# Fourteen instead of twelve of 125 edge tiles take their source columns by copies

## The reference, cut to what matters

```
h_nodes = silu(x @ Wn1 + bn1) @ Wn2 + bn2
h_edges = silu(edge_attr @ We1 + be1) @ We2 + be2
msgs = silu(concat[h_nodes[dst], h_nodes[src], h_edges] @ Wm1 + bm1) @ Wm2 + bm2
agg = segment_sum(msgs, dst) / max(counts, 1)
out = layernorm(x + upd) * g + b,   upd = silu(concat[x, agg] @ Wu1 + bu1) @ Wu2 + bu2
result = layernorm(x + out)
```

## Time and profile before

| | |
|---|---|
| median of the runs | 3641.66 us |
| profiled execution | 3643.69 us, span 3641.8 |
| GpSimd busy | 2698.5 us (74%) |
| VectorE busy | 2735.3 us (75%) |
| ScalarE busy | 2995.1 us (82%) |
| TensorE busy | 2794.5 us (77%), granted clock 0.76 on average |
| chain that ended last | GpSimd 64%, issue 21% |

### The profile page before, as it was taken

How to read it: one execution, slowest core, us unless ns; L and a number is a source line. 1 busy time by engine, 2 the same in 40 slices (tenths; PEclk the granted TensorE clock), 3 DMA queues, 4 the chain that set the end, 5 groups by cost and what they waited for, 6 DMA issues and landing times.

```text
span 3641.8 us, 93892 instructions
## 1 busy us (share of the span) xinstructions
PE 2794.5 (77%) x16224; PEld 2174.9 (60%) x16224; DVE 2735.3 (75%) x20847; ACT 2995.1 (82%) x23073; POOL 2698.5 (74%) x2848
## 2 busy tenths in 40 slices
PE   4878778777877788787777778777777787887785
PEld 2666556555666566666655556565655565665564
DVE  4778778778678677777687787786787877777876
ACT  3998888888888888888888888888888888888885
POOL 4777777777777777777777777777777777777774
PEclk7777777778777777777687787777777777677776
DMA  7444444444444444444454444444444444444442
GB/s 218 95 100 98 86 91 95 94 101 95 92 98 87 92 100 91 98 101 87 88 103 86 100 95 94 97 89 89 101 91 98 101 88 93 88 94 100 95 94 44
DMA packets 257330, 350.11 MB, mean 96 GB/s; under 512 B 105688, under 2 KB 193069, under 8 KB 246862
## 3 DMA queue, kind: packets, MB, share of 16 engines
q1 hardware_dynamic: 163340, 245.92, 31.8%
q0 software_dynamic: 91424, 95.97, 14.3%
q10 hardware_dynamic: 1954, 2.14, 0.2%
HBM read 330.76 MB, written 13.01 MB: 94 GB/s over the span
## 4 chain that ended last, share of the span: by engine, by line
POOL 64%; issue 21%; PE 8%; DMA 4%; DVE 2%; ACT 0%; DVEq 0%; SPq 0%; POOLq 0%; ACTq 0%
POOL b_ring L800 64%; DMA b_ring<-b_table,src 4%; PE p_pre L686 2%; PE p_pre L692 2%; PE p_sum L706 1%; PE p_hid L815 1%; DVE colbuf L632 1%; DMA work<-in_xT 1%; PE p_pre L695 0%; DVE comb L902 0%; PE p_last L958 0%; PE p_hid L378 0%; PE p_last L959 0%; DMA b_table<-to_ab 0%; DVE stats L995 0%
## 5 line engine op out<-in xcount | busy, mean ns | idle before, releaser
L800 POOL DMA_INDIRECT b_ring<-b_table,src x2825 | 2676.1, 947 | 865.8 <-issue 850.2
L632 ACT COPY colbuf<-shared 64x4 uint8 x21134 | 2128.0, 190 | 152.1 <-issue 140.7
L632 DVE COPY colbuf<-shared 64x4 uint8 x17511 | 1375.4, 194 | 282.2 <-issue 275.6
L686 PE MATMUL p_pre<-wa_ring,comb 128*128 128x64 f32 x6250 | 1027.7, 325 | 0.0
L686 PEld LDWEIGHTS p_pre<-wa_ring,comb 128*128 128x128 f32 x6250 | 979.2, 241 | 1.0 <-issue 1.0
L692 PE MATMUL p_pre<-b_ring,ident 128*128 128x320 f32 (+1 forms) x1250 | 575.3, 552 | 490.8 <-DMA b_ring<-b_table,src 488.3
L717 ACT ACTIVATE comb<-p_hid,b_e 64x320 f32<-64x320 f32 x1250 | 652.8, 522 | 359.8 <-PE p_hid L815 346.4
L902 DVE SCALAR_TENSOR_TENSOR comb<-shared,p_const 64x640 f32<-64x640 int32 x625 | 554.1, 887 | 506.2 <-PE p_pre L686 420.8
L706 PEld LDWEIGHTS p_sum<-hot_ring,msg 128*65 128x65 f32 x6250 | 579.8, 178 | 476.5 <-DVE agg L912 280.7
L706 PE MATMUL p_sum<-hot_ring,msg 128*65 128x64 f32 x6250 | 641.3, 267 | 278.4 <-DVE agg L912 171.6
L692 PEld LDWEIGHTS p_pre<-b_ring,ident 128*128 128x128 f32 x1250 | 295.5, 250 | 691.1 <-DMA b_ring<-b_table,src 577.2
(11 more groups left out here) (106 smaller groups left out, 592.4 us busy)
## 6 DMA issues: line engine op xcount, KB each, us to landing
e_ring<-in_edgeT SPq DMA_DIRECT2D x250, 320.0 KB
shared<-in_dst_row SPq DMA_DIRECT2D x125, 640.0 KB
b_ring<-b_table,src POOLq DMA_INDIRECT x2825
e_ring<-in_edgeT SPq DMA_DIRECT2D x50, 400.0 KB
shared<-in_dst_row SPq DMA_DIRECT2D x25, 800.0 KB
wa_ring<-a_table SPq DMA_DIRECT2D x625, 16.0 KB
work<-in_xT SPq DMA_DIRECT2D x25, 250.0 KB
work<-in_x SPq DMA_DIRECT2D x25, 250.0 KB
```

Of the source, the lines that this page charges most:

```text
L632: end = copy(colbuf[:, special % COLBUF, at:at + 1].bitcast(U8), of[j])
L686: return eng.matmul(p_pre[:, i % 2, k * H:(k + 1) * H], comb[:, i % COMBS, k * P:(k + 1) * P], wa_ring[:, i % RING, :], start=k == 0, stop ...
L800: eng.indirect_dma_start(b_ring[:, b_slot(i), k, :], None, b_table, bass.IndirectOffsetOnAxis(ap=src[:, u * TILES + k:u * TILES + k + 1], ...
```

## The change

SPECIAL has 14 units of a round instead of 12; of a special tile's 128 columns VectorE copies 61 instead of 58 and ScalarE 67 instead of 70. colbuf has 7 slots instead of 4, and VectorE's list has room for 40 words a unit instead of 32. In VectorE's loop the load of the list and the copies are done in two parts, the one-hot (hot) and the addition standing between them; before, both one-hots stood first, then one load and all copies, then the addition.

```diff
-SPECIAL = [1, 3, 5, 7, 9, 11, 13, 15, 17, 19, 21, 23]
-COLS = dict(vector=58, scalar=70)
-COLBUF = 4
+SPECIAL = [1, 2, 4, 6, 8, 9, 11, 13, 15, 17, 18, 20, 22, 24]
+COLS = dict(vector=61, scalar=67)
+COLBUF = 7
 LEADIN = 4
 HALF_AT = 13
 LIST_AT = (21, 8)
-LOAD = dict(vector=32, scalar=40)
+LOAD = dict(vector=40, scalar=40)
...
                 comb_of(i + AHEAD)
-            hot_of(i)
             if j in (0, HALF_AT):
                 wait_alone(eng, list_in[j // HALF_AT], 32 * rr + 32)
-            starts_v = loaded_columns(eng, "vector", j + LEADIN)
-            copied_columns(eng, "vector", eng.tensor_copy, j + LEADIN, starts_v).then_inc(col_ok["vector"], 1)
+            starts_v = loaded_columns(eng, "vector", j + LEADIN, 0, 2)
+            copied_columns(eng, "vector", eng.tensor_copy, j + LEADIN, starts_v, 0, 2)
+            hot_of(i)
             if i >= ADD_LAG:
                 add_sums(i - ADD_LAG)
+            starts_v = loaded_columns(eng, "vector", j + LEADIN, 1, 2)
+            copied_columns(eng, "vector", eng.tensor_copy, j + LEADIN, starts_v, 1, 2).then_inc(col_ok["vector"], 1)
             step(i)
```

## The result

The changed kernel takes 3695.51 us (median of four runs, 3693.84 to 3696.32), the kernel before beside it 3641.15. The ratio is 1.0148, with an interval from 1.0131 to 1.0166: slower by 54 us. I had forecast 3583, faster by 59 us, and a range up to 3622. Both the sign and the range were wrong.

What follows compares the result with a forecast made beforehand. GpSimd's row of 2825 gathers at 1.251 us was taken as the bound. From the profiled 3643.7 us, -62.5 for 50 gathers and +3 at the end gave 3584.2, stated as 3583 against the median; range 3577 to 3622.

Steps and rivals of the forecast that it cites:

- gaps 0.4: 4.67 us: VectorE's unit: comb 0.89, hot 0.49, addition 0.22, copies 2.68 and 0.4 us of load gaps make 4.67 us.
- 4.27 to 5.47: Bounds on VectorE's time a unit in us, with load gaps from 0 to 1.2 us; a round of 123.8 to 153.8.
- break-even: Round time of the other engines, 137.8 us, above which they pass GpSimd's span of 3579 and each us costs 25.
- 0.88 for "faster": Chance that the whole kernel gets faster: 0.70 forecast, 0.16 rival 1 or part of rival 2, 0.02 rival 3.
- -62.5 us: On GpSimd, 50 gathers fewer at 1.251 us each, all on the path while GpSimd waits for nobody.
- 134 + 25 r: Kernel time if the other engines need r us a round: start at about 102 us, 25 rounds, 38 at the end.
- Rival 1: VectorE's two list loads show, 0.63 us of gap a unit, r = 139.5: 3622 us; chance 0.16 with part of rival 2.
- Rival 2: ScalarE and VectorE take turns setting the pace, neither working ahead: 141.9 us a round, 3682 us; in full or with rival 1, 0.07 slower, 0.05 same.
- TensorE's slow units: TensorE's units of 6.1 us at a granted clock of 0.50, over GpSimd's 5.56; expected to be made good.
- The leads: 25 and 16 more copies ahead of the loop delay TensorE's first unit 2 to 3 us, hidden from GpSimd.
- The end's +3: At the last unit ScalarE and VectorE may be 0 to 10 us behind; 3 us added.
- Rival 3: GpSimd's gathers get dearer beside more VectorE copies; 1% growth gives back 35 us, 3618 us; chance 0.02.

Runs made afterwards that it cites:

- two experiments: The changed kernel with six copies a unit fewer on VectorE, 3605.48 us; and with VectorE's second load cut to four words, all copies kept, 3603.39 us.
- 57 and 71: The changed kernel with 57 of 128 columns on VectorE and 71 on ScalarE instead of 61 and 67: 3640.20 us; with the update also spread, 3616.77 us.

## Why the prediction was wrong, step by step

**The step that failed** is "gaps 0.4: 4.67 us" for VectorE's unit. Measured is (142.95 - 17)/25 = 5.04 us: inside the 4.27 to 5.47 that I had bounded, and above the break-even, 137.8 less 17 over 25, 4.83. The mechanism was in the sum, and the term is mis-sized in two parts. The gap was 431.6/625 = 0.69 us, not 0.4. A copy took 1743.9/21486 = 81.2 ns, not 78.5: 34.16 x 2.7 ns = 0.09. Together 0.38, which is the difference of 0.37 but for rounding. I had taken 0.44 from the earlier trace rows as the nearest row, but that is the average for one load of 28 words, and of an engine that waited 420.8 us for TensorE and so didn't set the pace. What tells of one that does is its gap behind comb and the price of a load by its words: two loads of 1.35 + 1.10 us, address arithmetic seven times 0.09 (the records of VectorE's queue), and 37 instructions to push at some 0.04 us (an estimate from the spaces between those records) come to about 4.6 us a unit in the sequencer. The engine's own work is 4.4 (0.89, 0.49, 0.21 and 34.16 x 0.0812). Neither hides the other in full: in the two places counted, the sequencer was six and eight instructions ahead when a load started. Together they make 5.04.

The chances failed with it. With half of the bounds (4.83 to 5.47) beyond the break-even, 0.88 for "faster" was not what my own bounds said. Their upper end, 153.8 us a round, gives 134 + 3845 = 3979, and my range stopped at 3622.

**Sum, term by term.** The gathers' -62.5 us was right in mechanism and size, and shows wherever VectorE gets out of the way (139.8 a round in two experiments, 27 of 31 us for thirteen tiles). Then the time comes back. The first of ScalarE's update activations moved from 281.3 to 288.6 us, the last from 3618.9 to 3670.6: 7 us in the first round and 44 in the other 24, 52 in all, which is the difference of the spans. With r = 142.95 my 134 + 25 r gives 3708, 14 above the span. It counts the update once too often: no update falls into the first round, and the last one runs alone in the 38 us at the end. With 17 us less it gives 3691, against 3693.4. So the break-even is r = 138.5 and not 137.8 (4.86 us a unit), and rivals 1 and 2 should have read 3605 and 3665.

**ScalarE** was right: busy 3251 us (3240 forecast), a unit 5.1 us between its activations (2007.46 to 2012.55), its longer load hidden. The Trainium skill's figure of 8 queued instructions (Advanced Engine Details and Errata, section Engine Queue Depths) I had weighed on ScalarE, where it changed little. The traces bear it out where it counts: VectorE's load at 2007.2 starts with seven unfinished copies and comb ahead of its first user, and in the run with the load ahead of comb six unfinished copies covered it. Weighed on VectorE it would have spoken against this change.

**TensorE, the leads, the end.** TensorE's slow units did not set the pace: with VectorE out of the way the rounds went at GpSimd's. The leads cost nothing: TensorE's first identity product runs at 99.34 us, 99.30 before. The end's +3 has no meaning with another bound.

**Rival 1** (VectorE's two loads show) is what happened, at a higher price: 0.69 of gap, not 0.63, and dearer copies; 3622 was forecast for it and 3695 measured. I had given it and a part of rival 2 a chance of 0.16, and only up to 3634. **Rival 2** had a number close by (3682), for a reason that the changed kernel doesn't have: with 8 copies a unit fewer on ScalarE the round stays at 142.9. Its mechanism exists at 57 and 71. **Rival 3** fell: 947 ns a gather, with 23% more copies on VectorE going on beside them. The Trainium skill (GPSIMD Engine Reference, section Specifications) speaks of contention between the two where VectorE's instruction is in a 2-port mode or has two inputs in SBUF. More copies beside the gathers brought none; whether a copy is of that kind no run here shows.

**What was to show it.** x2775 gathers at 1.25 us: yes. GpSimd's waits under 10 us: no, 103. TensorE's waits for gathers: none left. VectorE's issue before copies: 431.6 us, over the 0 to 400 that I gave, and its busy time 3123.7, not 3045. "Wrong if GpSimd waits for p_pre by tens of us; then r is over 138, and the engine without idle time names the rival": that is how it came, but for one word. VectorE has idle time in the page's sense, 20 us of the round; it has none that it waits for another.

**What stays open.** How much of the changed kernel's loss is the new order's (one load and one block of copies were not tried with 14 tiles at 61 and 67), how much the update's lumps add at that share, and what made six runs 29% slower.

## What to carry to other kernels

Give an engine's sequencer a row of its own in the sum: loads into registers, address arithmetic and the pushing of many tiny instructions. An engine that is 85% busy and waits for no one can be at its limit, as VectorE was here, and a gap that you read while it still had slack can grow when the slack is gone: 0.44 us became 0.69. Move work from the bound only as far as the next engine's full round allows: taking one tile of 125 out of the gathers gave 27 us here, taking two cost 54, and with a share that spared VectorE and the update spread two gave 24.

## What the runs showed of the hardware that I had not expected

- A load into VectorE's registers costs its sequencer about 0.06 us a word: 0.34 us for 4 words, 1.10 for 16, 1.35 for 20, 1.85 for 28. In these traces it was covered by the instructions queued when it started, some six to eight, and by no others. Placed ahead of the one long instruction of a unit, not behind it, it made the kernel 10.7% slower than before, where the changed kernel is 1.5% slower.
- A copy of 64 x 4 bytes on VectorE took 78.5 ns in one block of 28 (18970 of them 77.8 with thirteen tiles and the old order) and 81 to 83 ns in blocks of 12 to 20, where it is done in two blocks a unit.
- The same program took 3640 to 3657 us on most occasions and 4680 to 4695 (medians) on three, with 1.00 us of idle time between two instructions that waited for nothing. No cause is shown.
